# One order over all steps for a fused attention and routed feed-forward layer: float32 transposes ahead of the split, operands laid out by DMA, the mask added on TensorE

## The chip, the cores and the metric

One core of one Trainium2 chip runs the whole layer in one launch. The metric is the device time in microseconds of that core, from the start to the end of one execution. Engines are called as the profile calls them: PE (TensorE), DVE (VectorE), ACT (ScalarE), POOL (GpSimd) and SP (SyncE, which here only issues DMAs).

## What is computed

The input x is 4 batches of 1024 tokens of 256 features, float32. With xn the layer norm of x, the output is x + attention(xn) + ffn(xn).

```python
x = inputs @ W_qkv + b_qkv                       # 4096 tokens x 768
x = x.reshape(B, 16, S, 48); q, k, v = split(x, 3, axis=-1)   # heads of 16 features
qk = einsum('bhse,bhte->bhst', q, k) * 512 ** -0.5
attn = softmax(qk + triu(-inf, k=1)); sa = (attn @ v).reshape(B, S, 256)
attention = sa @ W_out + b_out
light = gelu(rms_norm(xn) @ w1_l + b1_l) @ w2_l + b2_l
s = xn @ routing_token                           # a score for each token
for _ in range(50): a = c - 0.1 * logsumexp((s + b) / 0.1); b = -relu(s + a)
chosen = top 256 tokens of each batch by exp((s + a + b) / 0.1)
ffn = light, plus at the chosen tokens gelu(rms_norm * w1_h + b1_h) @ w2_h + b2_h
```

The reshape to heads does not transpose: head h of a batch is 64 consecutive tokens by 768 features, read as 1024 rows of 48. There are 64 (batch, head) pairs, each a causal attention over 1024 rows with 16 features. The scores q.k need more than bfloat16 holds, so q and k are each split into three bfloat16 pieces (first, second and third part), and six products of pieces are added by laying the pieces side by side along the contraction: 6 x 16 = 96 rows.

## The kernel before

**Front.** 32 tiles of 128 tokens: ACT normalises a tile, PE transposes it and multiplies it with W_qkv (L945), DVE adds the bias (L1262), and SP stores the tile of qkv to the tensor qkv_d in HBM (L583). Tiles 16 to 31 have the first ring of attention work beside them.

**Steps.** The attention goes in 16 steps of 4 heads (256 tokens of qkv). In step q, PE computes the scores of the heads of step q for the exponentials (L1023, 39 items "E", PSUM banks psE), ACT takes the exponential into SBUF strips (L817), POOL zeroes the upper triangle of the diagonal blocks (L1690, "CAUSAL"), and PE multiplies with the values (L1041, 12 groups "PV" of four heads each in its own 32 columns of the array). One step ahead, the row maxima of the heads of step q+1 are found: PE computes the scores a first time (L986, 12 chunks "C" for each head, three PSUM slots psM), and DVE takes the largest of each row. A chunk that holds a diagonal block is masked by DVE in the same instruction (L1314: add maskrow, take the maximum, followed by an accumulator read); the others are a plain reduction (L1317). The negated maxima are split by POOL (L1602 to L1607, "MAX"), transposed by PE (L992, "MT"), copied (L1325) and written by a small DMA as three more contraction rows of the operand QT (L606), so that L1023 gives scores minus maximum.

**Operands.** For a step, a DMA loads 128 x 32 x 48 float32 from qkv_d into pm (L591). ACT casts the first pieces, each written three times (L763, two instructions), POOL computes the second and third pieces (L1573, L1577, L1584, five instructions "SUB"), all in bfloat16 pairs packed in 32-bit words of parts. PE then transposes parts, 32 transposes of 128 x 96 words for each step (L978, 8 items "T" of four), and DVE copies each item to QT (L1305). ACT copies the values to vext (L768).

**Order.** Each engine runs its instructions in the order written. The ring of a step is a list by hand (`ring_orders`); `merge` interleaves it with the E and PV items by a small model of costs; every steady step repeats the same order, padded with a NOP item so that the three slots come out even. `timeline` inserts the items of the other engines. The routing iterations (R on PE, L1002; three in a step) and the bisection rounds for the 256th score (S, L1006; five in each of the first two steps, three in the step before the last and four in the last) sit in the ring. At the head of the first step, the score column s_tok is stored to s_d four bytes at a time (L620), read back by two kinds of loads (L652, L654), and DVE reduces it (L1359) at an early place of its order.

**After the steps** come the output projection with the light feed-forward network (L1095 to L1137), the choice of the 1024 routed tokens, and the heavy network for them (L1206, L1219).

Of the kernel before, what the change touches and what calls it, by code (L numbers as in the profile page):

```python
# [28 lines left out]
P = 128  # L29
# [3 lines left out]
N_ITERS = 50  # L33
# [9 lines left out]

def ring_orders():

    C = lambda c, a, b: [("C", c, k) for k in range(a, b)]
    T = lambda c: [("T", c, 0), ("T", c, 1)]
    first = (T(0) + T(1) + C(0, 0, 12) + T(2) + C(1, 0, 6) + [("MT", 0)] + C(1, 6, 12) + T(3)
             + C(2, 0, 6) + [("MT", 1)] + C(2, 6, 12) + C(3, 0, 6) + [("MT", 2)] + C(3, 6, 12))
    steady = (T(0) + [("MT", 3)] + T(1) + C(0, 0, 8) + [("OT", 0), ("OT", 1)] + C(0, 8, 10) + [("R", 0)]
              + C(0, 10, 12) + T(2) + C(1, 0, 6) + [("MT", 0)] + C(1, 6, 10) + [("R", 1)] + C(1, 10, 12) + T(3)
              + C(2, 0, 6) + [("MT", 1)] + C(2, 6, 10) + [("R", 2)] + C(2, 10, 12)
              + C(3, 0, 6) + [("MT", 2)] + C(3, 6, 12))

    until = (5, 10, 13)

    def with_search(ring, rounds, at, apart):

        ring = list(ring)
        for k, n in enumerate(rounds):
            ring.insert(at + (apart + 1) * k, ("S", n))
        return ring

    first += [("NOP",)] * (len(first) % 2)

    second = [with_search(steady, range(until[0]), 17, 8), with_search(steady, range(until[0], until[1]), 4, 12)]
    before_last = with_search(steady, range(until[1], until[2]), 4, 20)
    steady += [("NOP",)] * (-len(steady) % MS)
    last = [("MT", 3), ("OT", 0), ("OT", 1)]
    routes, rounds = [("R", k) for k in range(5)], [("S", n) for n in range(until[2], ROUNDS)]
    while routes or rounds:
        last += routes[:1] + rounds[:1]
        routes, rounds = routes[1:], rounds[1:]  # L80
    return first, second, steady, before_last, last

# [5 lines left out]
EXPS = ([(kb, (c,), h * 512, 512 - h * kb * P) for kb in range(2) for c in range(4) for h in range(2)]  # L88
# [13 lines left out]
NPV = len(PVS)  # L102

TAKES = {0: (6, -1), 1: (7, -1), 2: (5, -1), 3: (0, 0), 4: (1, 0), 5: (2, 0), 6: (3, 0), 7: (4, 0)}

# [9 lines left out]
LOAD_M = 2.2  # L118
PACE, PRODUCT_LATER = 3.0, 0.4

def merge(ring, late, load):

# [1675 lines left out]
```

## Time and profile before

| | us |
|---|---|
| median of 3 runs | 921.78 (920.5 to 921.98) |
| profiled execution | 923.62 |
| its span (first to last instruction) | 921.8 |
| PE / DVE / ACT / POOL busy in the span | 813.1 / 632.2 / 473.2 / 456.1 |
| mean granted TensorE clock | 0.958 |

The busy time of PE holds modelled ends of pipelined matmuls, so a busy PE is not a PE at its peak. An instruction of 512 bfloat16 columns is listed with some 0.39 us, and yet the next one starts 0.23 us later. What an instruction occupies is therefore read from the distance between starts, or from the chain of waits, which counts only the part that moves the end. A step can be told by the copy of its outputs (L827): the first of the 15 starts at 211.1 us, the second at 260.3, then 335.14 and 409.96 two steps apart each, 634.44, and the last at 749.1; the copy of the sixteenth step is L870 at 777.3.

### The profile page before, as it was taken

How to read it: one execution, taken by the hardware profiler on the slowest of the kernel's cores; microseconds unless marked ns; L12 is line 12 of the kernel's file. 1: busy time of each engine (PE TensorE's matmuls, PEld its weight loads, DVE VectorE, ACT ScalarE, POOL GpSimd, SP SyncE). 2: the span in 40 equal slices, each digit the busy share in tenths (PEclk: the TensorE clock that was granted, in tenths of full speed). 3: DMA queues.
4: the chain of work that ended last, by engine and by line, in shares of the span. 5: the costliest groups of instructions: out<-in, count | busy, mean ns of one | idle time of the engine just before them, and what ended most of it. 6: DMA issues, size and time to landing. Idle time of an engine off the chain costs nothing.

```text
span 921.8 us, 14758 instructions
## 1 busy us (share of the span) xinstructions
PE 813.1 (88%) x4839; PEld 402.8 (44%) x4839; DVE 632.2 (69%) x1924; ACT 473.2 (51%) x972; POOL 456.1 (49%) x955
## 2 busy tenths in 40 slices
PE   4889983788899999999999999999999978998897
PEld 2455541334343343434434434334444423876465
DVE  5626772576779888898888898988878830263511
ACT  1242332345566676676767766667665646221320
POOL 3391400765753746637446465374654547134322
PEclk9899996797999999999999999999999999998999
DMA  9554423114030220202202112022010131554122
GB/s 287 175 161 149 138 95 53 35 38 97 3 47 3 48 42 8 48 5 45 49 3 48 15 36 47 3 48 44 6 14 4 14 74 33 147 187 133 46 23 23
DMA packets 170858, 56.95 MB, mean 62 GB/s; under 512 B 140448, under 2 KB 165664, under 8 KB 170784
## 3 DMA queue, kind: packets, MB, share of 16 engines
q1 hardware_dynamic: 160992, 52.35, 23.2%
q0 software_dynamic: 1536, 2.10, 1.4%
q10 hardware_dynamic: 8256, 1.57, 0.9%
q8 instruction: 39, 0.64, 0.3%
q14 instruction: 35, 0.29, 0.1%
HBM read 31.09 MB, written 22.04 MB: 58 GB/s over the span
## 4 chain that ended last, share of the span: by engine, by line
PE 56%; DVE 15%; ACT 9%; POOL 9%; issue 4%; DMA 4%; SPq 3%; DVEq 0%; POOLq 0%; ACTq 0%
PE ps L1041 13%; PE ps L986 9%; PE ps L1023 8%; ACT strips L817 7%; DVE ps L1314 6%; PE ps L945 6%; PE ps L978 4%; DVE mx L1317 4%; PE ps L1206 3%; PE ps L1137 3%; PE ps L1219 3%; DMA s_d<-s_tok 2%; PE ps L1095 2%; SPq L574 1%; PE ps L992 1%
## 5 line engine op out<-in xcount | busy, mean ns | idle before, releaser
L817 ACT ACTIVATE strips<-ps 128x512 f32<-128x512 f32 (+2 forms) x624 | 321.9, 577 | 232.6 <-PE ps L1023 228.7
L1314 DVE CUSTOM_DVE_ANT_0 ps<-ps,maskrow 128x128 f32<-128x128 f32 (+3 forms) x512 | 246.3, 503 | 36.1 <-PE ps L986 33.9
L986 PE MATMUL ps<-QT 96*128 96x512 bf16 (+3 forms) x768 | 230.8, 341 | 6.4 <-DVE mx L1314 3.6
L1023 PE MATMUL ps<-QT 99*128 99x512 bf16 (+3 forms) x768 | 216.8, 342 | 11.9 <-DMA QT<-mT 11.6
L1317 DVE TENSOR_REDUCE mx<-ps 128x1 f32<-128x512 f32 x256 | 176.0, 688 | 38.8 <-PE ps L986 37.1
L1041 PE MATMUL ps<-strips,vext 128*32 128x512 f32 (+3 forms) x1536 | 169.4, 515 | 7.5 <-POOL strips L1690 7.5
L1690 POOL TENSOR_SCALAR_AFFINE_SELECT strips<-strips 128x512 f32<-128x512 f32 x128 | 81.1, 636 | 164.7 <-ACT strips L817 164.5
L986 PEld LDWEIGHTS ps<-QT 96*128 96x128 bf16 x768 | 70.8, 98 | 177.0 <-issue 55.2
L1023 PEld LDWEIGHTS ps<-QT 99*128 99x128 bf16 x768 | 75.3, 104 | 73.1 <-ACT strips L817 25.4
L1305 DVE COPY QT<-ps 96x512 f32<-96x512 f32 x128 | 82.4, 677 | 11.8 <-PE ps L978 11.4
L978 PE MATMUL ps<-ident,parts 128*96 128x128 f32 x512 | 75.4, 282 | 5.9 <-DVE mx L1317 3.2
L1573 POOL TENSOR_TENSOR parts<-pm,parts 128x1024 bf16<-128x1024 f32 x32 | 76.0, 2378 | 4.3 <-ACT parts L763 4.3
L1314 DVE DVE_READ_ACCUMULATOR2_ANT mx<- 128x1 f32 x512 | 72.1, 141 | 0.0
L978 PEld LDWEIGHTS ps<-ident,parts 128*96 128x96 f32 x512 | 58.5, 129 | 24.8 <-DVE mx L1317 5.6
L763 ACT ACTIVATE parts<-pm 128x1536 bf16<-128x1536 f32 x32 | 59.2, 1916 | 3.1 <-DMA pm<-qkv_d 3.1
L945 PE MATMUL ps<-shared,xT 128*128 128x384 f32 (+1 forms) x128 | 50.0, 539 | 8.4 <-ACT xT L749 8.4
L1602 POOL CAST mW<-nm 128x8 bf16<-128x8 f32 x64 | 12.3, 192 | 90.6 <-DVE nm L1323 90.6
L1041 PEld LDWEIGHTS ps<-strips,vext 128*32 128x32 f32 x1536 | 31.0, 110 | 50.3 <-issue 33.5
L945 PE MATMUL ps<-shared,xrT 128*128 128x384 f32 (+1 forms) x128 | 46.7, 490 | 0.0
L1584 POOL TENSOR_TENSOR parts<-r,parts 128x512 bf16<-128x512 f32 x32 | 40.4, 1284 | 0.2
L1738 POOL TENSOR_TENSOR pm<-pm,shared 128x1024 f32<-128x1024 f32 x8 | 18.8, 2354 | 40.1 <-DMA pm<-in_L_attn_inputs 40.0
L1577 POOL TENSOR_TENSOR r<-pm,parts 128x1024 f32<-128x1024 f32 x16 | 38.2, 2386 | 0.0
(163 smaller groups left out, 918.7 us busy)
## 6 DMA issues: line engine op xcount, KB each, us to landing
qkv_d<-shared SPq DMA_DIRECT2D x32, 384.0 KB, 2.3
pm<-qkv_d SPq DMA_DIRECT2D x14, 768.0 KB, 8.0
sa_d<-pmo SPq DMA_DIRECT2D x16, 256.0 KB, 5.5
QT<-sa_d SPq DMA_DIRECT2D x8, 512.0 KB, 5.2
pm<-in_L_attn_inputs SPq DMA_DIRECT2D x8, 512.0 KB, 6.0
out<-QT SPq DMA_DIRECT2D x8, 512.0 KB, 3.3
strips<-in_L_attn_inputs SPq DMA_DIRECT2D x1, 2304.0 KB, 17.0
xrT<-xT SPq DMA_DIRECT2D x16, 128.0 KB, 2.4
```

What stands on the lines that cost most here:

```text
L763: nc.scalar.activation(partsb[:, u, :, g0:g0 + 3, :, t], src, ACT.Copy).then_inc(cast_done, 1)
L817: nc.scalar.activation(dst, src, ACT.Exp, scale=SCALE).then_inc(exp_done, 1)
L945: mm = pe.matmul(psA[u][:, h, 0:n], transposed(t, u)[:, k, :], w_qkv[:, k, HW * h:HW * h + n], start=(k == 0), stop=(k == KE - 1))
L978: mm = pe.transpose(psM[0:W, s, b * P:(b + 1) * P], parts[:, fu, n * W:(n + 1) * W], ident[:, :])
L986: mm = pe.matmul(psM[:, s, 0:n], QTb[0:W, fu, c * 1024 + qb * P:c * 1024 + (qb + 1) * P, 0], QTb[0:W, fu, c * 1024 + k0:c * 1024 + k0 + n, ...
L1023: mm = pe.matmul(psE[:, (NE * u + j) % ES, k * n:(k + 1) * n], QTb[0:W + 3, u, c * 1024 + kb * P:c * 1024 + (kb + 1) * P, 1], QTb[0:W + 3, ...
L1041: mm = pe.matmul(psO[32 * c:32 * c + 32, h, q0 - 512 * h:512], vext[:, u, 8 * c + kb, :], strip_at[kb][:, c, q0 - kb * P:q0 - kb * P + n], ...
L1305: nc.vector.tensor_copy(QT[0:W, fu, q0:q0 + 512], psM[0:W, s, :]).then_inc(free[s], 1)
L1314: nc.vector.tensor_tensor_reduce(psM[:, s, 0:n], psM[:, s, 0:n], maskrow[:, 512 - n:512], 1.0, MASKED, ALU.add, ALU.max, acc).then_inc(fre ...
L1317: nc.vector.tensor_reduce(acc, psM[:, s, 0:n], AX.X, ALU.max).then_inc(free[s], 1)
L1573: pool.tensor_tensor(dst, x_, p1, ALU.subtract).then_inc(split_done, 1)
L1690: pool.affine_select(out=diag, in_=diag, pattern=[[0, 4], [1, P]], compare_op=ALU.is_ge, fill=0.0, base=0, channel_multiplier=-1).then_inc ...
```

## The change

It has five parts.

1. *Transposes ahead of the split.* The float32 q and k are transposed before they are split. A DMA in four pieces loads q and k of a step into qk (128 x 8 x 4 x 32); PE transposes eight blocks of 128 x 128 (two items "T" of four); ACT copies each half to bfloat16 (the first piece, "P1"), DVE subtracts it ("R1"), POOL rounds the rest and subtracts again ("SPLIT", two instructions for each half). The result is `pieces`, 128 x 3 x 1024 bfloat16.
2. *Operands by DMA.* `pieces` is stored to HBM (768 KB) and loaded again by twelve DMAs (1.5 MB in packets of 2 KB) into two bfloat16 operands, QTq and QTk, which hold three steps each. The values are loaded by a DMA of their own straight into vext. The 8 copies L1305, the two casts L763 and the copy L768 go.
3. *Mask by TensorE.* A chunk with a diagonal block gets a second product, identity x maskb, accumulated on its last 128 columns. DVE then takes a plain maximum of every chunk.
4. *One order.* `schedule()` replaces `ring_orders`, `merge` and `timeline`: a list simulation of the five engines with all 16 steps in it, from which each engine's whole order comes, SP's too. Routing iterations and search rounds are spread over all steps. There is no NOP, and the maxima and the exponentials may be more than one step apart.
5. *Scores out and in.* s_tok is transposed on PE ("ST") and stored as 32 rows of 512 bytes. The maxima are transposed as bfloat16. 38 instead of 39 exponentials in a step cover the same columns.

The tail is the same but for the places of its buffers.

```diff
+TERMS = ((0, 2), (0, 1), (0, 0), (1, 0), (2, 0), (1, 1))
+FIRST = ([("T", f, h) for f in range(2) for h in range(2)]
+         + [x for c in range(4) for x in
+            [("C", 0, c, k) for k in range(6)] + ([("MT", 0, c - 1)] if c else []) + [("C", 0, c, k) for k in range(6, 12)]])
...
+def schedule():
...
+            if choice:
+                start = max(now[engine], min(c[0] for c in choice))
+                pick = min((c for c in choice if c[0] <= start + SOON),
+                           key=lambda c: c[1] + LATER * max(0.0, c[0] - start) + backlog(engine, c[2][0], start))
...
@@ sync
+            def load_qk(f):
+                if f > 0:
+                    s, at = place["T", f - 1, 1]
+                    sp.wait_ge(full[s], at + 1)
+                for u in range(2):
+                    sp.wait_ge(qkv_st[u], 16 * (f + 1))
+                for c in range(4):
+                    sp.dma_start(qk[:, :, c, :], pm_rows[f:f + 1, :, 8 * c:8 * c + 8, 0:2 * D]...).then_inc(qk_land, 16)
+            def load_v(q):
...
+                sp.dma_start(vext[:, q % 2, :, 0:D], pm_rows[q:q + 1, :, :, 2 * D:3 * D]...).then_inc(v_in[q % 2], 16)
+            def store_pieces(f):
+                sp.wait_ge(piece_done, 4 * f + 4)
+                sp.dma_start(pieces_d[f], pieces[:, :, :]).then_inc(pieces_st, 16)
+            def load_pieces(f, part):
+                if part == 0:
+                    sp.wait_ge(pieces_st, 16 * (f + 1))
+                    if f >= 3:
+                        sp.wait_ge(qk_ps, NE * (f - 2))
+                rows = pieces_d[f].rearrange("(c y d) k n -> y k d c n", c=4, y=2)
+                for n in range(4 * part, 4 * part + 4):
+                    y, i = n // len(TERMS), n % len(TERMS)
+                    operand = (QTq, QTk)[y][D * i:D * (i + 1), f % 3, :].rearrange("d (c n) -> d c n", c=4)
+                    sp.dma_start(operand, rows[y, TERMS[i][y]]).then_inc(qk_in[f % 3], 16)
+            for t in range(NT):
                 store_qkv(t // 2, t % 2)
+                if t == 4:
+                    load_qk(0)
+                elif t == 6:
+                    load_v(0)
...
+                elif t == 11:
+                    store_pieces(0)
+                elif t == 12:
+                    for part in range(3):
+                        load_pieces(0, part)
...
@@ scalar
+                nc.scalar.activation(pieces[:, 0, h * 512:(h + 1) * 512], psM[:, s, :], ACT.Copy).then_inc(p1_done, 1)
@@ tensor
-                        mm = pe.transpose(psM[0:W, s, b * P:(b + 1) * P], parts[:, fu, n * W:(n + 1) * W], ident[:, :])
+                        mm = pe.transpose(psM[:, s, b * P:(b + 1) * P], qk[:, 4 * h + b].rearrange("p c f -> p (c f)"), ident[:, :])
...
+                    mm = pe.matmul(psM[:, s, 0:n], QTq[0:W, f % 3, ...], QTk[0:W, f % 3, ...], start=True, stop=not diagonal)
+                    if diagonal:
+                        mm = pe.matmul(psM[:, s, n - P:n], identb[:, :], maskb[:, :], start=False, stop=True)
@@ vector
-                    if diag:
-                        nc.vector.tensor_tensor_reduce(psM[:, s, 0:n], psM[:, s, 0:n], maskrow[:, 512 - n:512], 1.0, MASKED,
-                                                       ALU.add, ALU.max, acc).then_inc(free[s], 1)
-                    else:
-                        nc.vector.tensor_reduce(acc, psM[:, s, 0:n], AX.X, ALU.max).then_inc(free[s], 1)
+                    nc.vector.tensor_reduce(acc, psM[:, s, 0:n], AX.X, ALU.max).then_inc(free[s], 1)
+                    nc.vector.tensor_tensor(r1[:, h, :], psM[:, s, :], pieces[:, 0, ...], ALU.subtract)   # R1
@@ gpsimd
+                pool.tensor_copy(pieces[:, 1, halves], r1[:, h, :]).then_inc(piece_done, 1)
+                pool.wait_ge(piece_done, 4 * f + 2 * h + 1)
+                pool.tensor_tensor(pieces[:, 2, halves], r1[:, h, :], pieces[:, 1, halves], ALU.subtract).then_inc(piece_done, 1)
```

In the front of the changed kernel, PE's T items of the first step stand ahead of tile 8 and those of the second ahead of tile 14, and the chunks of the first step begin with tile 16 as before, behind a wait for all twelve operand loads. On SP, load_qk(1) follows tile 9, load_v(1) tile 15, store_pieces(1) and load_qk(2) tile 17, and the operand loads of the second step tile 19.

## Rows read from the trace of the kernel before

**Rows 1.** Busy time by stage: length, engines (instructions), clock, DMA share, GB/s.
```profile
0.00:60.00 60.00, 38.89 (x115) 22.20 (x116) 30.59 (x100) 16.57 (x29) 28.23 (x61) 0.91 0.68 213
60.00:139.10 79.10, 73.20 (x292) 42.98 (x290) 55.79 (x139) 25.59 (x44) 25.56 (x77) 1.00 0.41 134
139.10:211.10 72.00, 46.47 (x274) 20.16 (x275) 37.23 (x113) 27.20 (x56) 34.83 (x93) 0.79 0.25 50
211.10:260.50 49.40, 43.60 (x256) 20.15 (x256) 36.12 (x111) 26.51 (x55) 29.85 (x75) 0.83 0.17 29
260.50:297.90 37.40, 35.23 (x244) 15.07 (x243) 32.78 (x102) 25.35 (x53) 21.23 (x41) 1.00 0.19 30
634.60:749.10 114.50, 105.35 (x710) 44.39 (x709) 93.89 (x293) 67.93 (x150) 60.48 (x142) 0.97 0.11 16
749.10:777.30 28.20, 23.85 (x167) 8.78 (x166) 2.24 (x8) 20.09 (x54) 18.02 (x55) 0.94 0.32 85
777.30:921.80 144.50, 129.31 (x602) 93.43 (x602) 48.34 (x153) 35.68 (x69) 47.13 (x45) 0.97 0.34 89
```

**Rows 2.** Chain of waits, one steady step: start us, duration us, what.
```profile
by line: PE ps L1041 21.7%; PE ps L986 14.9%; ACT strips L817 13.7%; PE ps L1023 12.5%; DVE ps L1314 8.8%; PE ps L978 6.9%; DVE mx L1317 6.4%; issue 4.4%; PE ps L992 2.3%; ACT osb L827 2.3%; PE ps L1002 2.2%; DVE mx L1314 1.2%; DVE mT L1325
...
416.17 0.88 PE ps L978 x8
...
417.22 0.06 PE ps L986
417.28 0.23 PE ps L1023
417.50 1.00 PE ps L1041 x8
...
432.98 0.36 PE ps L1041 x8
```

**Rows 3.** DVE in the same step, by start; x2 is two instructions.
```profile
421.45 0.69 DVE L1317 TENSOR_REDUCE mx<-ps 128x1 f32<-128x512 f32 x1
422.06 0.42 DVE L1314 CUSTOM_DVE_ANT_0 ps<-ps,maskrow 128x256 f32<-128x256 f32 x1
...
426.37 1.27 DVE L1305 COPY QT<-ps 96x512 f32<-96x512 f32 x2
427.57 0.28 DVE L1314 CUSTOM_DVE_ANT_0 ps<-ps,maskrow 128x128 f32<-128x128 f32 x1
...
427.77 0.46 DVE L1314 CUSTOM_DVE_ANT_0 ps<-ps,maskrow 128x256 f32<-128x256 f32 x1
...
428.67 0.73 DVE L1314 CUSTOM_DVE_ANT_0 ps<-ps,maskrow 128x512 f32<-128x512 f32 x1
...
429.32 0.68 DVE L1317 TENSOR_REDUCE mx<-ps 128x1 f32<-128x512 f32 x1
```

**Rows 4.** Groups by shape: busy us, mean ns | idle before, releaser.
```profile
L763 ACT ACTIVATE parts<-pm 128x1536 bf16<-128x1536 f32 x32 | 59.2, 1916 | 3.1 <-DMA pm<-qkv_d 3.1
...
L1573 POOL TENSOR_TENSOR parts<-pm,parts 128x1024 bf16<-128x1024 f32 x32 | 76.0, 2378 | 4.3 <-ACT parts L763 4.3
```

**Rows 5.** PE's timeline, first step: idle time in brackets, with its releaser.
```profile
154.71 0.59 PE L1023 MATMUL ps<-QT 99*128 99x512 bf16 x1 [9.74 <-DMA QT<-mT]
...
163.99 0.39 PE L1009 MATMUL ps<-ident 128*24 128x128 f32 x1 [7.42 <-DVE mx L1317]
```

**Rows 6.** DMA issues of the run: count, KB each, median us to landing.
```profile
pm<-qkv_d SPq DMA_DIRECT2D x14, 768.0 KB, 8.0
...
s_d<-s_tok SPq DMA_DIRECT2D x1, 16.0 KB, 16.0
```

**Rows 7.** SP's DMA issues in a steady step: start us, us.
```profile
406.04 0.70 SPq L606 DMA_DIRECT2D QT<-mT  x1
413.26 0.37 SPq L628 DMA_DIRECT2D sa_d<-pmo  x1
413.81 3.12 SPq L591 DMA_DIRECT2D pm<-qkv_d  x1
```

More of the change, by code:

```diff
@@ L42 @@
 ROUNDS = 17
[L45 to L81, printed above, removed]
@@ L632, in step @@
[L632 to L644 removed]
+                sp.dma_start(dst[q:q + 1].rearrange("a p n f -> (a p) n f"),
+                             pmo[:, q % 2].rearrange("p c n f -> p (c n) f")).then_inc(sa_st[q % 2], 16)
@@ L832, in route_exp, with route_ln @@
                 nc.scalar.activation(re[:, :], rz[:, :], ACT.Exp, scale=1.0 / EPS_ROUTE, accum_out=rsum[:, :]).then_inc(re_done, 1)
[L834 to L835 removed]
+            def route_ln(r):
+                s, at = place["R", r]
                 act.wait_ge(full[s], at + 1)
                 nc.scalar.activation(lns[:, :], psM[:, s, 0:1], ACT.Ln).then_inc(free[s], 1)
[L839 to L853 removed]
@@ L856, in _ @@
-            nc.scalar.preload_act_table_set("natural_log_exp_and_others")
-            step(ring_second[0], (0, 0), 0, 0, late=False)
-            step(ring_second[1], (0, 1), 0, 1)
-            for i in range(1, NQ // 2 - 1):
-                step(ring_steady, (i, 0), i, 0)
-                step(ring_steady, (i, 1), i, 1)
-            li = NQ // 2 - 1
-            step(ring_before, (li, 0), li, 0, load=False)
-            step(ring_last, NQ - 1, li, 1, load=False, value=False)
-            act.wait_ge(pv_done, NPV * NQ)
@@ L868, in _ @@
-            s, at = ring_at(NQ - 1, ("OT", 1))
-            act.wait_ge(full[s], at + 1)
-            nc.scalar.activation(osb[:, :], psO[:, :, :].rearrange("p h n -> p (h n)"), ACT.Copy).then_inc(osb_done, 1)
+            nc.scalar.preload_act_table_set("natural_log_exp_and_others")
+            for item in order["Scalar"]:
+                if item[0] == "E":
+                    exps(item[1], item[2])
+                elif item[0] == "P1":
+                    first_piece(item[1], item[2])
+                elif item[0] == "OUT":
+                    outputs(item[1])
+                elif item[0] == "RX":
+                    route_exp(item[1])
+                elif item[0] == "R":
+                    route_ln(item[1])
@@ L958, in _, with ring_item @@
             tile_a(0, 1)
-            for i in range(1, FRONT_FROM // 2):
-                tile_a(i, 0)
-                tile_a(i, 1)
-            def ring_item(step, fi, fu, f, item, r=None):
-                s, at = ring_at(step, ("OT", item[1]) if item[0] == "SKIP" else item)
-                if not (isinstance(at, int) and at == 0):
+            def ring_item(item):
+                s, at = place[item]
+                if at > 0:
                     pe.wait_ge(free[s], at)
@@ L1636, in search @@
                                            ).then_inc(th, 1)
-            split(0)
+            for h in range(2):
+                split(0, h)
             for n in range(1, ROUNDS):
```

982 lines of the change are left out of this document (473 added, 509 removed), and 4 rows, old and new, of the table EXPS.

## Prediction

> **What bounds the kernel now.** I cut the span by the stages of the program first: a front of 139.1 us, sixteen attention steps to 777.3 us, and a tail of 144.5 us [rows 1]. The tail keeps its instructions and PE is busy in 129.3 of its 144.5 us, so the change can only matter before 777.3 us. Of this, thirteen steps (from the output copy at 260.3 us to that at 749.1) take 488.8 us, 37.6 us each, at the full granted clock but for two places. The first two steps take 121.4 us instead of 75, at a granted clock of 0.79 and 0.83 [rows 1]. The second view is the chain of waits through one steady step [rows 2]: only some six tenths of it are PE; ACT's exponentials have 13.7%, DVE's maxima 8.8% and 6.4%. So PE is nearly the bound, and loses time to its two partners in turn.
>
> The third view is what each engine is occupied with in a steady step. For PE I take the chain's own pieces [rows 2], where the modelled ends don't count: 0.23 us for 512 bfloat16 columns, 0.06 for 128, 1.00 for a value product of four heads at 512 columns and 0.36 at 128, 0.88 for eight float32 transposes. The two passes of scores have 36 x 512 columns each: 36 x 0.23 = 8.3 us, twice. The value products are twelve groups, six of 512 columns, two each of 384, 256 and 128: 6 x 1.00 + 2 x (0.78 + 0.57 + 0.36), the middle two put between the ends, = 9.4. The 32 operand transposes are 4 x 0.88 = 3.5; output transposes 0.9, the rest (maxima, routing, NOP) 0.8. Together 31.2 of 37.4 us. DVE shows 32.8 busy, ACT 25.4, POOL 21.2 [rows 1]. DVE is thus as full as PE, and three PSUM slots tie the two together. The 6.2 us in which PE isn't occupied are the size that the change can win in a steady step beyond its own work.
>
> **PE's own work.** Transposes: 32 become 8, 3.5 us become 0.9: minus 2.6. Each of 32 diagonal chunks gets a product of 128 columns: 0.06 us each [rows 2], plus 1.9. Bounds: 0, if it hides wholly, and 0.23 each, the price of a 512 column product, plus 7.4. I take 0.06, since that row is a product of just this width, with its own weight load, between two others. NOP and bfloat16 maxima transposes: minus 0.3. PE's work falls from 31.2 to 30.2 us; by itself it is worth one microsecond. The Trainium skill speaks against this part: "TensorE: Matmul & The Clock Gate", section "LDWEIGHTS (loading the stationary operand)", says that a weight load takes its number of columns over 1.2, so 107 ns for 128, whatever the contraction. If the loads of the identity and of the next chunk were paced so, the 32 products would cost 3.4 us instead of 1.9, and the sum below would be 20 us later. The trace has the next instruction 0.06 us after a 128-column product [rows 2], so here the loads do overlap, and I keep to that.
>
> **DVE.** Reading distances between starts [rows 3]: a pair of operand copies 1.20 us, so 8 copies are 4.8 us, all gone. Two subtractions R1 come in at the same 512 columns from PSUM, 0.60 to 0.70 each: plus 1.3. The masked maximum of 128 columns takes 0.20 us to the next start and of 512 columns 0.65; the plain one of 512 takes 0.61. The accumulator read of 0.14 us overlaps almost all. So dropping mask and read wins some 0.05 each, 1.6 us for 32 (bounds 0 and 32 x 0.14 = 4.5). DVE falls from 32.8 to 27.7 us.
>
> **ACT and POOL.** ACT loses two casts of 1.92 us [rows 4] and a copy of the values (some 0.5), and gains two copies of 512 columns, at the chain's pace for an exponential at most 0.6 each: 25.4 to 22.2. POOL loses L1573 twice, 4.8 us [rows 4], and the other three split instructions, with 1024 or 512 elements at the same rate some 4.9; it gains for each half a rounding and a subtraction of 512 elements, at half of L1573 1.2 each (bounds 0.4 and 2.4): 21.2 to 16.3. Neither is near PE.
>
> **What is late next.** With DVE 2.5 us below PE instead of 1.6 above it, and no step boundary at which everything waits for the last maxima, PE should be late for its own sake most of the time. Of the 6.2 us of waiting, some go with every switch between the kinds of products and stay: twelve value groups start 0.05 to 0.1 us later than a same-kind product would, about 1 us. I keep half of the whole, 3.2, as neither row nor rule gives the rest: bounds 1.2 (switches alone) and 6.2 (nothing won). The period is 30.2 + 3.2 = 33.4 us; 13 x (37.6 - 33.4) = 54.6 us less.
>
> **DMA and SP.** This is what has to hide all the above. For each step SP issued six DMAs: 3.12 us of queue for pm with its 4096 packets, 0.37 for the outputs, 0.70 for each of four maxima [rows 7], 6.3 us in all. It will issue 23: four for q and k and one for v, with 4096 packets each, at pm's rate 3.1 + 3.1; a store 0.4; twelve operand loads at 0.70, 8.4; the rest 3.2. That is 18.2 us, beside a wait of a few us for the store to land, in 33.4: covered. The DMA engines are busy in 0.19 of a step, 7.1 us [rows 1], nearly all of it for the 4096 packets of pm and as many of the outputs. There will be 4096 more small ones, 3.6 us more, and 2.3 MB in packets of 2 KB and 6 KB: at the front's 213 GB/s with a share of 0.68 [rows 1] this is 7.3 us. In all 18 of 33 us. The operands are three deep, so a load may be most of a step late before PE sees it. If this cover is gone, each microsecond of lateness in a step costs 15.
>
> **The first two steps.** Two stalls of PE stand here: 9.74 us for the maxima of the fourth head, whose DMA was issued behind the store of the score column, which landed after 16.0 us [rows 5, 6]; and 7.42 us, in which DVE waits for the scores read back and PE for DVE [rows 5]. The column is stored in 4096 packets of four bytes; transposed, it is 32 of 512 bytes, and should land in less than the 8.0 us of pm's 4096 packets [rows 6]. Ten search rounds on POOL and the low clock behind the stalls have the rest: PE is busy 90 us in 121.4, where two steady steps need 70. From the front's end, two steps of 33.4 us, some 2 us to the output copy as in a steady step, and 5 for a pipeline that fills and one read-back that is a little late, make 74 where 121.4 stood, and leave a gain of 47; I count 44, for a few microseconds at a low clock. Bounds: 25, if another stall of 10 us and the low clock behind it remain, and 52.
>
> **The front.** PE is idle for 5.9 us in its second part [rows 1], all waiting that less DVE work could end. Against it stand the twelve operand loads behind tile 12: SP issues nothing else for 12 x 0.37 to 12 x 0.70, 4.4 to 8.4 us [rows 7], with the stores of tiles 13 and 14 behind them. Those release the buffers of tiles 15 and 16, for which ACT and then PE wait. T items for two steps, 1.8 us, replace those for one, 3.5, and mask products add 1.9. I count 0, bounds minus 6 and plus 9. The last step (28.2 us) has no maxima beside it: 0.
>
> **Sum**, against the profiled execution: 923.6 - 54.6 - 44 + 0 = 825.0. That execution is 1.8 us above the median of the runs, 0.2%; I forecast 825 us.
>
> **Rivals.** *PE alone sets the pace.* For it speaks that DVE, ACT and POOL all end under 28 us a step. Waits fall to 1.4: 31.6 us a step, 13 x 6.0 = 78 less, 48 in the first two steps, 6 in the front: 792. Against it: order is fixed beforehand by rough costs, and any misjudged one makes PE wait.
>
> *Waits stay as they are.* If the 6.2 us come from fixed order and hand-over and not from DVE's load, the period is 30.2 + 6.2 = 36.4: only 15.6 less, with 40 at the start: 868. For it speaks that ACT, at 25.4 of 37.4 us by no means full, has nearly as much of the chain as DVE [rows 2].
>
> *Slower: SP's queue becomes the bound.* Its place is the order of DMAs on SP, in which operand loads, q, k, v and the small maxima follow one another, and L1023 waits for the last. The nearest other row for the price of a load that scatters is pm's 3.12 us [rows 7]. At that, twelve loads take 37.4 us, SP needs 47, and the steps last 47: 13 x (47 - 37.6) = 122 more, less 20 at the start: 1026. It decides for slower from a period of 37.6 + 44/13 = 41 us, that is from 2.6 us for each load. Against it: pm's 3.12 us go with 4096 packets, and an operand load has 64; the maxima with 24 packets take 0.70. The Trainium skill warns of such transfers: "DMA: Bandwidth & Descriptors", "Rules for kernel authors", counts anything under 64 KB as mostly overhead and asks for 128 partitions; these loads are 128 KB on 16 partitions. No row of this trace has such a one; by it alone I would give this rival more.
>
> **Chances.** Forecast 0.60 (own range 806 to 848), PE alone 0.13, waits stay 0.18, SP 0.07, and 0.02 for no change, by a mix of a stall and unchanged waits. The range 796 to 868 leaves out part of the second, half of the third and the slower case, some 2 in 10. A measurement tells 0.2%, 1.8 us, from no change; faster 0.91, same 0.02, slower 0.07.
>
> **What would show it.** Distances between output copies of 33.4 us; DVE near 27.7 us in each and PE's chain share above 0.75; starts 0.06 us behind the mask products; no idle stretch of PE over 3 us between 139 and 200 us, and a granted clock above 0.95 there; stores of tiles 13 and 14 late in the front. The prediction is wrong if L986 or L1023 wait for DMAs in the steady steps, if the chain still gives ACT and DVE a third, or if the clock is low in a stage where it now is 1.00.

## The result

The changed kernel takes 860.69 us (859.27 to 861.38, 4 runs) against 921.14 us (916.33 to 921.98) on the same chip: ratio 0.9352, interval 0.9316 to 0.9387. The forecast was 825 us with a range of 796 to 868; the time lies in the range, 36 us above the forecast. The sign came out as forecast, and so did the main mechanism: PE is held up less by its partners. The front did not, and the steps reach their sum in another way than forecast.

The busy times of the whole execution after, in the order of the profile's first part, and the chain:

```profile
PE 772.1 (90%) x4953; PEld 385.9 (45%) x4953; DVE 555.0 (65%) x1301; ACT 422.1 (49%) x940; POOL 358.9 (42%) x941
...
PE 70%; DVE 16%; DMA 3%; issue 3%; POOL 3%; SPq 2%; ACT 1%; DVEq 0%; POOLq 0%; ACTq 0%
```

DVE has fallen from 632 to 555 us, POOL from 456 to 359, and PE's share of the chain has risen from 56 to 70%. The span must again be cut by stages. The first column is the stretch in us, and the rest as in [rows 1].

```profile
0.00:60.00 60.00, 27.26 (x80) 15.67 (x81) 36.80 (x90) 9.73 (x20) 17.78 (x42) 0.92 0.65 184
60.00:169.10 109.10, 88.50 (x340) 51.01 (x338) 55.45 (x110) 22.76 (x50) 24.13 (x96) 0.93 0.62 153
169.10:217.30 48.20, 45.82 (x309) 19.22 (x310) 39.74 (x89) 29.63 (x68) 24.82 (x66) 0.96 0.77 136
217.30:252.00 34.70, 33.72 (x258) 15.05 (x257) 27.69 (x64) 22.66 (x56) 20.55 (x60) 1.00 0.96 163
427.40:462.00 34.60, 33.58 (x257) 15.19 (x256) 27.45 (x65) 22.92 (x55) 21.35 (x63) 1.00 0.56 91
665.50:690.90 25.40, 24.53 (x193) 9.42 (x192) 15.61 (x37) 16.64 (x32) 6.70 (x19) 1.00 0.21 23
690.90:711.60 20.70, 18.86 (x146) 5.84 (x145) 1.27 (x4) 17.04 (x36) 5.59 (x10) 1.00 0.43 116
711.60:859.60 148.00, 132.85 (x602) 94.90 (x602) 48.04 (x153) 35.79 (x69) 47.13 (x45) 0.94 0.33 87
```

With the end of the last projection (136.5 us before, 166.2 after) and the starts of the output copies as marks, the difference of 62.2 us between the two spans is this:

| stage | before | after | difference | forecast |
|---|---|---|---|---|
| front, to the end of the last projection | 136.5 | 166.2 | +29.7 | 0 (-6 to +9) |
| to the second output copy | 123.8 | 85.8 | -38.0 | -44 |
| 13 steps to the fifteenth copy | 488.8 | 438.9 | -49.9 | -54.6 |
| last step | 28.2 | 20.7 | -7.5 | 0 |
| tail | 144.5 | 148.0 | +3.5 | 0 |

So the attention steps gave 95 us, close to the 98.6 of the forecast, and the front, which was priced at nothing, took 30 us back. The tail's 3.5 us go with a granted clock of 0.90 from 770 us on (0.96 before in the like stretch). The tail's instructions are the same in all kernels below, and it takes some 148 us in `a_nomask`, `a_dvemask` and `a_best1` (clock 0.94) and 144.4 to 145.2 us in most others (0.96 or 0.97). Totals of two kernels can thus differ by 3 us without any cause in the steps, and the stage times below decide.

**The thirteen steps aren't alike.** These rows are the products for the maxima (L979) alone, by stretch: length, PE busy (products), their weight loads (one for each), clock, DMA share, GB/s.

```profile
166.20:217.30 51.10, 21.76 (x73) 7.11 (x72) 0.97 0.75 136
217.30:252.00 34.70, 13.86 (x48) 4.58 (x47) 1.00 0.96 163
252.00:565.20 313.20, 126.24 (x433) 40.26 (x432) 1.00 0.66 99
665.50:690.90 25.40, 7.67 (x26) 2.39 (x25) 1.00 0.21 23
```

In the kernel before (L986), the last of the thirteen:

```profile
710.10:749.10 39.00, 13.63 (x46) 4.05 (x45) 0.96 0.07 9
```

A full step has 48 of them. The nine steps from 252.0 to 565.2 us are full ones, and take 34.8 us each, where the kernel before has 37.4. The last of the thirteen has only 25 and takes 25.4 us (39.0 before, with 45): half a step of maxima was computed ahead, between 166.2 and 217.3 us, where 72 stand instead of 48. The 438.9 us are therefore not thirteen times a period, and their mean of 33.8 us is no distance between two steps.

**Where the front lost its time.** DVE's first instructions after, start and duration in us:

```profile
1.29 1.76 DVE L1210 MEMSET vext<- 128x2048 f32 x1 [1.29 <-PEq L1714]
...
5.88 10.30 DVE L1213 MEMSET QTk<- 3x12288 bf16 x1 [2.62 <-issue]
...
16.90 0.43 DVE L1224 BATCH_NORM_STATS2 bn<-strips 128x6 f32<-128x256 f32 x1
```

The memset of QTk's three rows of ones takes 10.30 us and stands ahead of the first statistics, for which ACT and then PE wait. In the kernel before these start at 4.09 us:

```profile
4.09 0.37 DVE L1243 BATCH_NORM_STATS2 bn<-strips 128x6 f32<-128x256 f32 x1
```

PE's timeline of the front, with idle time and its releaser in brackets:

```profile
22.63 1.09 PE L932 MATMUL ps<-ident,xr 128*128 128x128 f32 x4 [22.63 <-ACT xr L790]
...
40.60 0.69 PE L932 MATMUL ps<-ident,xr 128*128 128x128 f32 x2 [7.07 <-ACT xr L790]
```

```profile
96.00 5.50 PE L947 MATMUL ps<-shared,xT 128*128 128x384 f32 x8 [10.00 <-ACT xT L808]
...
135.40 2.66 PE L947 MATMUL ps<-shared,xrT 128*128 128x384 f32 x4 [4.52 <-DVE shared L1243]
```

The first matmul starts at 22.63 us, at 9.82 before. The 10.00 us before tile 15 are the wait that the prediction placed: SP issues the twelve operand loads from 80.87 to 86.57 us, and the copy of tile 13 to xrT only at 86.61, where ACT waits for it:

```profile
80.50 0.32 SPq L612 DMA_DIRECT2D qkv_d<-shared  x1
80.87 2.88 SPq L652 DMA_DIRECT2D QTq<-pieces_d  x6
83.79 2.78 SPq L652 DMA_DIRECT2D QTk<-pieces_d  x6
86.61 0.60 SPq L609 DMA_DIRECT2D xrT<-xT  x1
```

**A middle step.** The chain of waits after, from 427 to 463 us, a little more than one step:

```profile
by line: PE ps L1041 26.7%; PE ps L979 21.6%; PE ps L1023 16.9%; DVE mx L1291 16.6%; PE ps L982 3.3%; PE ps L972 2.9%; issue 2.8%; PE ps L997 2.6%; PE ps L1001 2.2%; DVE nm L1297 1.0%; PE ps L987 0.9%; POOL mW L1556 0.6%; POOL mW L1553 0.6%
...
427.86 0.07 PE ps L982
...
427.95 0.70 DVE mx L1291
...
431.50 0.06 PE ps L982
...
432.60 0.99 PE ps L1041 x8
...
438.31 1.30 DVE mx L1291 x2
...
439.74 0.06 DVE nm L1297
...
439.84 0.30 DVE mx L1291
...
446.55 1.76 DVE mx L1291 x3
```

The mask product takes 0.06 to 0.07 us in the chain (427.86, 431.50). PE's lines have over 75%, where [rows 2] has some six tenths, and ACT has left the chain. What is left is mostly DVE's: at the end of each head PE is held for 1.3 to 1.8 us of maxima (438.31, 446.55), and for the reduction of the head with the wait for its own results ahead of it (439.74, 439.84). One wait for a DMA stands in the thirteen steps, for a small one of the maxima, issued among the operand loads of a later step:

```profile
421.51 0.38 PE L1023 MATMUL ps<-QTq,QTk 99*128 99x512 bf16 x1 [1.35 <-DMA QTq<-mT]
```

### The profile page after: what moved, and what is told of

It reads as the page before. It is cut to its first block, busy times and chain, and to the rows that moved or that the text cites. A ratio compares the mean times of both kernels' runs of the same rounds, so it can differ in the third digit from the quotient of the medians.

```text
span 859.6 us, 14565 instructions
## 1 busy us (share of the span) xinstructions
PE 772.1 (90%) x4953; PEld 385.9 (45%) x4953; DVE 555.0 (65%) x1301; ACT 422.1 (49%) x940; POOL 358.9 (42%) x941
## 4 chain that ended last, share of the span: by engine, by line
PE 70%; DVE 16%; DMA 3%; issue 3%; POOL 3%; SPq 2%; ACT 1%; DVEq 0%; POOLq 0%; ACTq 0%
PE ps L1041 16%; PE ps L979 14%; PE ps L1023 12%; DVE mx L1291 11%; PE ps L947 7%; PE ps L1188 4%; PE ps L1119 3%; PE ps L1201 3%; PE ps L982 2%; DMA xrT<-xT 2%; PE ps L1081 2%; SPq L652 1%; PE ps L1115 1%; DVE shared L1243 1%; PE ps L997 1%
## 5 line engine op out<-in xcount | busy, mean ns | idle before, releaser
L1291 DVE TENSOR_REDUCE mx<-ps 128x1 f32<-128x512 f32 (+3 forms) x768 | 389.1, 551 | 109.5 <-PE ps L982 58.0
L839 ACT ACTIVATE strips<-ps 128x512 f32<-128x512 f32 (+1 forms) x608 | 312.3, 578 | 142.8 <-PE ps L1023 80.5
L979 PE MATMUL ps<-QTk,QTq 96*128 96x512 bf16 (+3 forms) x768 | 227.0, 331 | 8.5 <-DVE mx L1291 4.5
L1023 PE MATMUL ps<-QTq,QTk 99*128 99x512 bf16 (+3 forms) x768 | 195.6, 328 | 2.3 <-DMA QTq<-mT 1.4
L979 PEld LDWEIGHTS ps<-QTk,QTq 96*128 96x128 bf16 x768 | 72.6, 99 | 144.8 <-DVE mx L1291 78.7
L982 PE MATMUL ps<-maskb,identb 128*128 128x128 bf16 x512 | 110.4, 221 | 0.0
L1023 PEld LDWEIGHTS ps<-QTq,QTk 99*128 99x128 bf16 x768 | 66.6, 100 | 60.5 <-ACT strips L839 30.9
L982 PEld LDWEIGHTS ps<-maskb,identb 128*128 128x128 bf16 x512 | 50.5, 99 | 23.5 <-issue 5.3
L932 PE MATMUL ps<-ident,xr 128*128 128x128 f32 x64 | 13.1, 291 | 29.7 <-ACT xr L790 29.7
L1544 POOL TENSOR_TENSOR pieces<-r,pieces 128x512 bf16<-128x512 f32 x32 | 37.0, 1156 | 2.7
L1394 DVE TENSOR_TENSOR QTk<-ps,QTq 128x256 f32<-128x256 f32 x32 | 13.4, 422 | 33.7 <-PE ps L1119 33.6
L1119 PE MATMUL ps<-shared,strips 128*128 128x256 f32 x128 | 33.8, 388 | 0.0
```

The source lines that it names most:

```text
L839: nc.scalar.activation(dst, src, ACT.Exp, scale=SCALE).then_inc(exp_done, 1)
L979: mm = pe.matmul(psM[:, s, 0:n], QTq[0:W, f % 3, c * 1024 + qb * P:c * 1024 + (qb + 1) * P], QTk[0:W, f % 3, c * 1024 + k0:c * 1024 + k0 + ...
L982: mm = pe.matmul(psM[:, s, n - P:n], identb[:, :], maskb[:, :], start=False, stop=True)
L1023: mm = pe.matmul(psE[:, (NE * q + j) % ES, k * n:(k + 1) * n], QTk[0:W + 3, q % 3, c * 1024 + kb * P:c * 1024 + (kb + 1) * P], QTq[0:W + 3 ...
L1119: mm = pe.matmul(o, saT[:, t % 2, k * P:(k + 1) * P], wout[:, k, :], start=False, stop=(k == KE - 1))
L1291: nc.vector.tensor_reduce(acc, psM[:, s, 0:n], AX.X, ALU.max).then_inc(free[s], 1)
```

## The experiments

All ratios are against runs of the kernel before on the same chip; the stage times are those of the profiled runs.

### The front: the fill and the order of the loads

`a_memset` moves the fill to GpSimd, behind its first split at 59 us; there it takes 5.21 us as 32-bit words.

```diff
-            const(dve.memset(QTk[W:W + 3, :, :], 1.0))
...
             for h in range(2):
                 split(0, h)
+            pool.wait_ge(piece_done, 4)
+            const(pool.memset(QTk[W:W + 3, :, :].rearrange("p b w -> p (b w)").bitcast(I32), 0x3F803F80))
+            pool.wait_ge(consts, 17)
```

> The changed kernel with one edit: the ones in rows 96 to 98 of QTk are written by GpSimd as 32-bit words behind the first split, instead of by VectorE as its fourth instruction (10.30 us there). Theory A (the VectorE fill stands on the path of the first tile): the first TensorE instruction starts near 12 us instead of 22.6, and the run is 10 to 16 us shorter than the changed kernel's 860.7, about 847. Theory B (the front is paced by the loads of x and by SyncE's queue, so an earlier start is lost in a later wait): the first instruction is earlier, the end of the front stays at 169 us and the run at 858 to 861.

845.97 us, ratio 0.9172 (0.9132 to 0.9211), against 0.9352 (0.9316 to 0.9387) of the changed kernel. The first matmul starts at 9.65 us, and the front ends at 154.8 us, 11.4 earlier. Theory A holds: 11.4 of the 14.7 us are the front's, and 3.0 the tail's with its higher clock. The stages between are within 1.2 us of what they were.

`a_spread` issues the operand loads four behind each of three tiles:

```diff
-                elif t == 12:
-                    for part in range(3):
-                        load_pieces(0, part)
+                elif t in (12, 13, 14):
+                    load_pieces(0, t - 12)
...                                   # and likewise 19, 20, 21 for the second step
```

> The changed kernel with one edit: the twelve operand loads of the first and of the second step are issued four behind each of three tiles (12, 13, 14 and 19, 20, 21) instead of twelve behind one. Theory A (the 5.7 us in which SyncE issues nothing else hold back the stores of tiles 13 and 14, and through their buffers ScalarE and TensorE, idle for 10.0 us before tile 15): most of this stall goes, 5 to 9 us less, about 853. Theory B (it is the traffic of the loads ahead of the stores, not their issue): the same stall comes in smaller parts, and the time stays within 2 us of 860.7.

850.31 us, ratio 0.9235 (0.9207 to 0.9263); the front ends at 160.2 us, 6.0 earlier, and the tail has 3.2 us less. In PE's timeline the 10.00 us are now

```profile
89.77 4.54 PE L945 MATMUL ps<-shared,xT 128*128 128x384 f32 x8 [2.30 <-ACT xT L806]
...
99.79 0.27 PE L977 MATMUL ps<-QTk,QTq 96*128 96x128 bf16 x1 [5.26 <-DMA QTk<-pieces_d]
```

2.30 us behind the buffers, and then 5.26 us for the operands themselves, which the chunks of the first step wait for. The front's gain is in A's range of 5 to 9 us, and B's "same stall in smaller parts" didn't come: the second wait is a new one, for the landing of the operands. The rest of the total's 10.4 us is mostly the tail's.

`a_memset_spread` has both.

> Both edits in one kernel. If the two stalls are independent, the gains add: 15 to 25 us below the changed kernel's 860.7, about 838. If one uncovers the other, the gain is that of the larger edit alone, 10 to 14 us, about 848.

838.38 us, ratio 0.9106 (0.9082 to 0.9130), 22 us below the changed kernel: the front ends at 148.2, 18.0 earlier, where 11.4 and 6.0 make 17.4, and the tail has 144.9. Three fifths of the front's 30 us are these two edits.

### The steps: who holds PE

`a_short` takes each maximum over the first quarter of its chunk's columns and leaves the rest out, which is two fifths of DVE's work (16.87 us busy from 427.4 to 462.0 us, where the changed kernel has 27.45); nothing else is changed:

```diff
-                    nc.vector.tensor_reduce(acc, psM[:, s, 0:n], AX.X, ALU.max).then_inc(free[s], 1)
+                    nc.vector.tensor_reduce(acc, psM[:, s, 0:n // 4], AX.X, ALU.max).then_inc(free[s], 1)
```

> The changed kernel with each maximum taken over the first quarter of the columns of its chunk; nothing else is left out. VectorE falls from 27.5 to some 14 us in a step. Theory A (of the 34.5 us of a middle step, over TensorE's own 30.2, the greater part is waiting for VectorE at the ends of heads): steps of 31 to 32.5 us, a run of 820 to 835. Theory B (the rest is the fixed order and ScalarE, whatever VectorE does): steps above 33.5 us, a run above 850.

825.32 us (2 runs), ratio 0.8953 (0.8915 to 0.8991); 3.6 us of the gain are the tail's. The thirteen steps take 414.4 us, 24.5 less, and the nine full ones among them 32.8 us each, where the changed kernel has 34.8. The chain from 427 to 463 us is PE's alone:

```profile
by line: PE ps L979 28.7%; PE ps L1041 27.2%; PE ps L1023 27.0%; PE ps L982 6.1%; PE ps L993 3.3%; PE ps L997 2.9%; PE ps L972 2.5%; PE ps L1001 1.2%; PE ps L987 1.1%
```

So 32.8 us is, within some tenths, PE's own time with switches, routing and search, and 2.0 us a step is waiting for DVE. Theory A's total came, and its words only in part: of the 4.6 us by which a full step exceeds the forecast's 30.2, less than half is waiting for DVE. The rest is work of PE that the forecast hadn't priced.

`a_nomask` leaves out the mask products (`stop=True` for every chunk, no second product).

> The changed kernel without the 512 mask products of the maxima; the maxima are taken over the unmasked scores. Theory A (a mask product costs TensorE the 0.06 us between starts, and TensorE sets the pace): 32 x 0.06 = 1.9 us less in each of 15 steps and in the front, 25 to 32 us less than 860.7, about 832. Theory B (the pace is set by VectorE emptying three slots): under 10 us less.

853.84 us, ratio 0.9251 (0.9215 to 0.9287). The thirteen steps take 433.2 us, 5.7 less. In one of them, from 388.3 to 425.7 us, the wait for a small DMA of the maxima is 2.31 us instead of 1.35, the granted clock is 0.95 instead of 1.00, and the step is 1.7 us longer than in the changed kernel. The other twelve are shorter by 0.6 us each, where 32 products of 0.06 us are 1.9. Neither number of theory A came, and B's did: only a third of the work taken from PE shortens the step. That PE waits for DVE instead is inferred and not shown apart.

`a_dvemask` undoes the mask part:

```diff
-                    if diagonal:
-                        mm = pe.matmul(psM[:, s, n - P:n], identb[:, :], maskb[:, :], start=False, stop=True)
...
+                    if _d:
+                        nc.vector.tensor_tensor_reduce(psM[:, s, 0:n], psM[:, s, 0:n], maskrow[:, 512 - n:512], 1.0, MASKED,
+                                                       ALU.add, ALU.max, acc).then_inc(free[s], 1)
```

> The changed kernel with its mask part undone: no mask products, VectorE adds the mask and takes the maximum in one instruction as in the kernel before. Theory A (TensorE sets the pace, mask on TensorE costs more than it spares VectorE): 5 to 20 us less than 860.7. Theory B (the hand-over with VectorE sets the pace, where each masked maximum frees its slot only after the accumulator read): 5 to 25 us more, 866 to 886.

866.43 us, ratio 0.9398 (0.9360 to 0.9435), where the changed kernel has 0.9352 (0.9316 to 0.9387). The intervals of the ratios overlap; the thirteen steps of the profiled runs take 444.0 against 438.9 us. Of these 5.1 us, 2.7 are one step (392.7 to 431.2 us) with a wait of 2.50 us for the small DMA and a clock of 0.96; the other twelve are 0.2 us longer each. The mask on TensorE is worth 2 to 5 us in all: theory B, at its lower end, and half of it through that one step.

`a_plan2` only alters the order, by two costs of the schedule:

```diff
-TENSOR = {"T": 0.95, "MT": 0.12, "OT": 0.95, "R": 0.12, "S": 0.15, "ST": 0.25}
+TENSOR = {"T": 0.45, "MT": 0.12, "OT": 0.45, "R": 0.12, "S": 0.15, "ST": 0.25}
...
-            return 0.05 + 0.00113 * n + (0.2 if x[3] == 11 else 0.0)
+            return 0.05 + 0.00113 * n + (0.6 if x[3] == 11 else 0.0)
```

> The changed kernel with two costs of its schedule set to what the trace shows: four float32 transposes 0.45 us instead of 0.95, and 0.6 us instead of 0.2 for the end of a head on VectorE (the wait for its own last results and the reduction to nm). Only the order of the instructions changes. Theory A (misjudged costs at the ends of heads make TensorE run into full slots): steps shorter by 0.5 to 1.5 us, 7 to 20 us less than 860.7. Theory B (any order has these waits, as three slots can't cover them): within 4 us of 860.7, either way.

854.49 us (851.76 to 858.59), ratio 0.9273 (0.9227 to 0.9318). The thirteen steps take 427.9 us, 11 less, and the nine full ones 33.9 us each, 0.9 less, so A holds there. The total is only 6.2 us lower, under A's 7 to 20: the second step takes 41.3 us instead of 34.7, at a clock of 0.88, with this wait:

```profile
249.58 0.59 PE L1023 MATMUL ps<-QTq,QTk 99*128 99x512 bf16 x1 [3.84 <-DMA QTq<-mT]
```

SP issued the seven loads of the tail's weights in this step (234.2 to 237.8 us), q and k of a later step behind them, whose issue took 7.08 us (2.44 at 405 us in the changed kernel), and the maxima of the head only at 245.88. `a_best1` tests that, with the two edits of the front, those of `a_plan2`, and

```diff
-        return 2 * PACE
+        return 14 * PACE
```

for the place of these loads.

> The changed kernel with four edits: ones written by GpSimd, operand loads of the front spread over three tiles, the two costs of the schedule corrected as in the order run before, and the 2.1 MB of tail weights loaded late (ready at 14 paces of the schedule instead of 2). In the order run before, a 3.84 us wait for the small maxima DMA and a granted clock of 0.88 stood in the second step, where these weights are loaded. Theory A (the weights' load makes that wait, and the corrected order is worth 11 us over 13 steps): no such wait, the second step near 34 us, and 824 to 829 us in all, against 838.4 for the first two edits alone. Theory B (the small DMA waits behind the operand and q, k loads, not the weights): the wait stays, and the run takes 831 to 836.

825.62 us (823.43 to 830.56), ratio 0.8955 (0.8903 to 0.9007). The second step takes 33.7 us without such a wait, and the thirteen steps 427.9 again. Theory A holds. That the time meets the forecast of 825 us is chance: the front ends 11 us later than forecast, and the last step is 8.6 us shorter.

### The first two steps

`b_early` edits the kernel before: the score column goes out in seven parts beside the front.

```diff
+                if t in (17, 20, 23, 25, 27, 30):
+                    store_s(...)          # columns 0:6, 6:12, 12:18, 18:23, 23:27, 27:31; the last one behind tile 31
```

> The kernel before with one edit: the score column is stored in seven parts beside the second half of the front, the last one of one column, instead of in one part of 4096 packets behind it. Theory A (the 16.0 us landing of this store makes both stalls of the first step, and the low granted clock follows from them): the stalls of 9.74 and 7.42 us shrink to under 3 us each, the clock of the first two steps rises to 0.95 or more, and the run is 15 to 30 us under 921. Theory B (the search rounds and splits on GpSimd hold these two steps, and the low clock is theirs): the stalls shrink but the second output copy still comes near 250 us; under 12 us are won.

937.77 us, ratio 1.0204 (1.0167 to 1.0242): slower. Each part holds up the stores of qkv behind it; this one, from the chain, lands after 9.90 us, where 2.3 us are usual:

```profile
88.41 9.90 DMA qkv_d<-shared
```

PE is idle for 3.55 and 7.13 us in the front, which ends at 151.6 us, and the first step still has idle stretches of 4.23 and 8.73 us. Neither theory's number came; it doesn't decide between them, since the stalls stayed, but it shows what packets of four bytes do to the queue.

`b_scores` does part 5 alone in the kernel before: in the place of the front's NOP, PE transposes s_tok, DVE copies it, and SP stores 32 rows.

```diff
+                    pe.wait_ge(qkv_done, NT)
+                    mm = pe.transpose(psM[0:NT, s, 0:P], s_tok[:, :], ident[:, :])
...
+            sp.dma_start(s_d.rearrange("(t p) -> t p", p=P), sT[:, :]).then_inc(s_st, 16)
```

> The kernel before with part 5 alone: the score column is transposed on TensorE in the place of the front's NOP and stored as 32 rows of 512 bytes. Storing it in seven parts of 4-byte packets had only moved the stalls. Theory A (the two stalls of the first step, 17 us, and the low clock behind them come from the slow 4-byte store): the first idle stretch goes, the second falls to some 5 us, the first two steps take 95 to 105 us instead of 124 from the end of the projections, the run takes 893 to 905 us. Theory B (GpSimd, with splits and ten search rounds in these two steps, holds them anyway): under 12 us less than 921.

906.81 us, ratio 0.9831 (0.9790 to 0.9873). The store lands after 1.8 us instead of 16.0. What stood in [rows 5] with 9.74 and 7.42 us of idle time is now

```profile
149.12 0.39 PE L1014 MATMUL ps<-ident 128*24 128x128 f32 x1 [2.73 <-DVE mx L1326]
...
163.76 1.71 PE L1046 MATMUL ps<-strips,vext 128*32 128x384 f32 x16 [2.52 <-POOL strips L1700]
```

2.73 us at the NOP-like item of the first step, and the next stall is one for POOL's masking of the strips, which was there before as well. The second output copy comes at 244.0 instead of 260.3 us. That is 16.3 of the 38 us of this stage. The clock of the two stretches is 0.94 and 0.93, where [rows 1] has 0.79 and 0.83, and yet they take 107.3 us from the end of the projections, 32 more than two steady steps. Both theories missed by little: A's 893 to 905 us and 95 to 105 us for the two steps, and B's gain of under 12. The stalls and most of the low clock were the store's, as A says. In what is left PE waits 12.5 us for POOL, 8.6 for the strips and 3.9 for the maxima, which fits B; the changed kernel has 0.2 us of it in this stage. That the other 22 us of the stage come from the spread of the search rounds and the lighter splits is an inference from this and wasn't tried alone.

### A version that beats both

`a_best2` adds to `a_best1` that ACT writes the transposed tiles 0 to 15 straight to xrT:

```diff
-                    sp.wait_ge(xT_done, 2 * i + u + 1)
-                    sp.dma_start(xrT[:, :, bass.ds((2 * i + u) * P, P)], xT[:, u]).then_inc(xc_st[u], 16)
...
-                    act.wait_ge(qkv_ps, t - 1)
-                    act.wait_ge(xc_st[u], 16 * i)
```

> As the kernel with four edits, and in the front ScalarE writes the transposed tiles 0 to 15 straight into xrT as it does with 16 to 31, without the double buffer xT, the 16 DMAs from it and the waits for them. Theory A (these waits are what holds the first half of the front: idle stretches of 6.5, 3.8, 2.7 and 2.3 us, each behind such a DMA): 10 to 16 us less than the kernel with four edits. Theory B (the x loads and the operand path are late anyway, and the chunks of the first step wait for them): 3 us less or nothing.

818.78 us (816.76 to 819.37), ratio 0.8873 (0.8836 to 0.8910), against 0.8955 (0.8903 to 0.9007). The front ends at 141.5 us, 5.9 earlier: between the theories. The waits for these copies are gone, and 8.04 us stand ahead of the first chunk for the operands, where 5.24 us were. The tail's higher clock gives 3.1 us besides.

### How thick the cover of the DMAs is

`a_double` adds to the changed kernel, behind each operand load of steps 2 to 15, a second one to a scratch tensor:

```diff
+                    if f >= 2:
+                        sp.dma_start(again_d[f, n], rows[y, TERMS[i][y]]).then_inc(again, 16)
```

> The changed kernel with each operand load of steps 2 to 15 followed by a second one of the same 128 KB, which goes to a scratch tensor in HBM; nothing waits for these but the end. Twelve more DMAs for each step: 5.4 us more of SyncE's queue at 0.45 us each, and the share of busy DMA engines in a middle step, 0.56 to 0.73 now, rises by 0.15 to 0.25. Theory A (the transfers lie in cover): within 4 us of 860.7. Theory B (the small DMAs of the maxima, which L1023 waits for, are behind them, as the weights' load showed in one order): waits of L1023 for QTq<-mT in the steps, 10 us more or above.

861.78 us, ratio 0.9336 (0.9311 to 0.9362): the same in total, because two differences cancel. The thirteen steps take 442.6 us, 3.7 more, and the tail 3.1 us less at its higher clock. Twelve of the thirteen steps are within 0.1 us of what they were. One is 3.5 us longer, at a clock of 0.91, behind

```profile
422.04 0.56 PE L1028 MATMUL ps<-QTq,QTk 99*128 99x512 bf16 x1 [1.81 <-DMA QTq<-mT]
```

It is the step that has the wait of 1.35 us in the changed kernel. So the transfers lie in cover, which is thin in one step. The busy share of the DMA engines, expected to rise by 0.15 to 0.25, didn't: over the nine full steps it is 0.63 instead of 0.66, while they move 146 instead of 99 GB/s. That share is thus no measure here of how much more they could take.

## Why the prediction was right, and where not

**PE's own work.** Right on the mask product, and too low in the sum. The mask product takes 0.06 us in the chain, as the row of a 128-column product said. The Trainium skill ("TensorE: Matmul & The Clock Gate", section "LDWEIGHTS (loading the stationary operand)") gives 107 ns for a load of 128 columns; the trace doesn't agree that products would be paced so, with its 0.06 us. PE's own time in a step, forecast as 30.2 plus 1.2 of switches, is 32.8 us by the full steps of `a_short`. The difference of 1.4 us is mostly one term: maxima transposes, routing and search together were carried on at 0.5 us (0.8, less 0.3 for part 5). In the chain of `a_short` their lines (L987, L997, L1001) have 5.2%, or 1.7 us of 32.8. Two things went wrong there. The line of [rows 2] already gives L992 and L1002 4.5% of a step, 1.7 us, and not 0.8. And the change spreads the search rounds over the steps and runs four routing iterations in a full step instead of three, which the working left out.

**DVE, ACT and POOL.** Forecast 27.7, 22.2 and 16.3 us a step. A middle step, 427.4 to 462.0 us, has 27.45, 22.92 and 21.35 busy. DVE and ACT are right. POOL is not to be compared at once, since search rounds and more routing iterations now fall in this step; a rounding takes 0.61 and a subtraction 1.16 us, where both were forecast at 1.2.

**What is late next.** Forecast 33.4 us a step; the full steps take 34.8. The mean of all thirteen, 33.8, is nearer to the forecast, and that is luck: the last of them takes 25.4 us because half of its maxima had been computed ahead, which the prediction didn't expect. Thirteen steps of 34.8 us would have given 36 us instead of the 49.9 measured and the 54.6 forecast. The waits themselves were well guessed. Of the 3.2 us that the working kept, 1.2 were switches, which no run shows apart, and 2.0 other waits; `a_short` shows 2.0 us for DVE. That choice of a half was a guess between bounds. That waits for ACT would go, as they did, wasn't in the working, and no run shows which part of the change removed them. The rival "PE alone" wanted 31.6 us. `a_short` has 32.8 in full steps and `a_plan2` 33.9, so even without waits this order doesn't reach it; correcting two costs of the schedule won back 0.9 of the 2.0 us. "Waits stay" had 36.4 us a step and 868 us in all; its total is nearer to the measured one, but ACT's waits did not stay.

**DMA and SP.** Forecast: covered. Right for the steps, by `a_double`, but for one wait of 1.35 us: an operand load costs SP 0.45 to 0.48 us (2.69 to 2.88 for six), not 0.70 or pm's 3.12. The DMA engines are busy in 0.56 to 0.73 of a middle step, 0.66 in the mean of nine, where 0.55 was forecast. In the front and in one order with the weights' load the cover wasn't there.

**The first two steps.** Forecast -44, measured -38. The stalls behind the score column are 16.3 us of it, against 17.2 of idle time in the rows. The working then let the low clock and POOL's load vanish together, which they nearly did (clock 0.96 and 1.00). The stage also bears 120 products for the maxima, where the forecast's two steps have 96, with DVE's work on them; what these cost here wasn't measured apart.

**The front: the step that failed.** It was priced at 0 with a bound of +9, and cost 29.7. One term was missing. The change adds a fill of three rows of 12288 elements at the head of DVE, and the prediction doesn't name it. It costs 10.30 us itself and 12.8 at the first matmul, of which 11.4 to 12 come out at the end of the front. The second term was named, and its place was right: loads behind tile 12, waits at tile 15. Its size was off, since it counted SP's issue alone (4.4 to 8.4 us), and not that the copy of tile 13 must still land behind 1.5 MB: 8.84 us in the chain from issue to landing, where the median of such a copy before was 2.4. The whole stall is 10.0 us. Without these two terms the changed kernel is `a_memset_spread`, 839.4 us in the profiled execution. The 14.4 us from there to 825.0 are the front, which still ends 11.7 us late, the first two steps with 5 and the thirteen with 5, less 7.5 that the last step gives back. Of the front's 11.7 us, `a_best2` shows 6 to be waits for the copies to xrT. The other 5 stay in it, beside the wait of 8.04 us for the operands, and weren't taken apart.

**The last step.** Forecast 0, measured -7.5 (28.2 to 20.7 us). The prediction took it over from the kernel before, and overlooked that part 4 spreads the search rounds: the four that stood in it, eight recorded products of PE (1.77 us busy) with POOL's work between them, are gone. POOL's busy time in it falls from 18.0 to 5.6 us, PE's idle time from 4.3 to 1.8, and the granted clock is 1.00 instead of 0.94. It has 41 score products for the exponentials (L1023) instead of 44, and all 96 value products, as before. How the 7.5 us divide among these wasn't tried.

## What to carry to other kernels

Where a DMA is moved into a queue in front of a double-buffered stage, count its issue, and the landing of what comes behind it, against the slack of the buffers. Two engines that are nearly equally full hold each other up: taking work from the one in front (the mask from PE) gave a third of its price, while from the other it gave what the wait was. An order made from a cost list is worth checking against distances between starts in the trace. And when the order is free to run ahead, count the items in each step before taking a mean of steps for a period.

## What the runs showed of the hardware beyond that

- A DVE memset of 3 partitions by 12288 bfloat16 took 10.30 us, one of 128 partitions by 2048 float32 1.76 us. GpSimd wrote the same bytes as 3 by 6144 words in 5.21 us.
- Stores with packets of four bytes hold up what follows in the queue also in small parts: in `b_early`, seven of 0.5 to 3 KB cost the front 15 us, and a store of qkv behind one took 9.90 us to land instead of 2.3. The same 16 KB in 512-byte packets landed in 1.8 us.
- The same step has a wait of PE for a small DMA in five kernels. Where it is 1.35 (changed kernel) and 1.45 us (`a_short`), the granted clock of the step is 1.00; where it is 1.81 (`a_double`), 2.31 (`a_nomask`) and 2.50 us (`a_dvemask`), it is 0.91, 0.95 and 0.96. Whether the wait made the clock fall wasn't tried.
